# Summing four gathered corners with one tensor_reduce in place of two additions

## The reference

```python
xo = g_lt * gather(qltx, qlty) + g_rb * gather(qrbx, qrby) + g_lb * gather(qltx, qrby) + g_rt * gather(qrbx, qlty)
```

## Time and profile before

| | |
|---|---|
| times shown, us | 7589.84, 7599.73, 7600.01 |
| median, us | 7599.73 |
| span of the profiled execution, us | 7593.5 |
| busy PE / DVE / ACT / POOL, us | 5859.6 / 4572.4 / 2753.9 / 5492.1 |

### The profile page before, as it was taken

The page is one execution under the profiler, slowest core; times in us unless marked ns, Lnnn a source line. Parts: engine busy times, 40 slices in busy tenths (PEclk is TensorE's granted clock), DMA queues, the critical chain, the costliest instruction groups (busy, mean ns, idle before and its releaser), DMA issues.

```text
span 7593.5 us, 104067 instructions
## 1 busy us (share of the span) xinstructions
PE 5859.6 (77%) x33682; PEld 2811.5 (37%) x33682; DVE 4572.4 (60%) x7421; ACT 2753.9 (36%) x5357; POOL 5492.1 (72%) x5044
## 2 busy tenths in 40 slices
PE   3578787788788788888888887887888878867666
PEld 2333333334333333344334443333333433332323
DVE  3366566566666766656665666667666566755541
ACT  2333333334333343434433343333434344332322
POOL 0177777777777777777777777777777777777760
PEclk7788898899888889988888998988999888988777
DMA  2222232222322323222332223223232233312120
GB/s 88 63 71 60 57 81 72 65 82 67 84 69 70 86 68 95 64 68 76 78 81 64 83 67 84 69 68 88 65 98 64 61 82 78 81 50 66 49 65 22
DMA packets 424825, 540.78 MB, mean 71 GB/s; under 512 B 310746, under 2 KB 318974, under 8 KB 417646
## 3 DMA queue, kind: packets, MB, share of 16 engines
q0 software_dynamic: 161280, 330.62, 16.6%
q1 hardware_dynamic: 262980, 203.17, 10.4%
HBM read 404.04 MB, written 116.94 MB: 69 GB/s over the span
## 4 chain that ended last, share of the span: by engine, by line
POOL 32%; PE 31%; issue 16%; DVE 14%; ACT 5%; DMA 1%; DVEq 1%; SPq 0%; POOLq 0%; ACTq 0%
POOL gath L584 32%; PE pair L1002 10%; PE ring L940 4%; PE ring L859 3%; PE ps_def L1023 2%; ACT u L1034 2%; PE ps_acc L976 2%; DVE prod L1578 2%; DVE gath L1596 2%; ACT prod L1234 1%; DVE gath L1602 1%; PE ring L904 1%; PE ring L805 1%; PE ring L915 1%; PE ring L821 1%
## 5 line engine op out<-in xcount | busy, mean ns | idle before, releaser
L584 POOL DMA_INDIRECT gath<-table_d,idx_all x5040 | 5491.9, 1090 | 1872.7 <-issue 1871.5
L1002 PE MATMUL pair<-clamp_x,tab 128*128 128x392 f32 (+1 forms) x5760 | 2793.7, 588 | 922.7 <-DVE prod L1578 895.9
L1578 DVE SCALAR_TENSOR_TENSOR prod<-prod,pair 128x392 f32<-128x392 f32 (+1 forms) x2880 | 1629.2, 569 | 1861.0 <-PE pair L1002 1806.5
L1234 ACT ACTIVATE prod<-ps_y,y_bias 128x392 f32<-128x392 f32 (+1 forms) x2880 | 1480.9, 597 | 2250.6 <-PE ps_acc L976 2199.6
L1002 PEld LDWEIGHTS pair<-clamp_x,tab 128*128 128x128 f32 x5760 | 1044.4, 210 | 2292.1 <-DVE prod L1578 1561.1
L1596 DVE TENSOR_TENSOR gath<-gath,wgt 128x1152 f32<-128x1152 f32 x560 | 756.9, 1352 | 368.6 <-DMA gath<-table_d,idx_all 367.9
L1034 ACT ACTIVATE u<-ring 128x448 f32<-128x448 f32 (+7 forms) x1376 | 603.4, 480 | 948.5 <-PE ring L904 244.5
L976 PE MATMUL ps_acc<-prod,w_samp 128*32 128x392 f32 (+1 forms) x5760 | 649.4, 523 | 6.5 <-DVE prod L1578 6.5
L1023 PE MATMUL ps_def<-xt,w_samp 32*32 32x224 f32 x5760 | 392.8, 438 | 140.3 <-DVE xt L1611 140.3
L1554 DVE TENSOR_SCALAR clamp_x<-ps_x 128x392 f32<-128x392 f32 (+1 forms) x720 | 410.4, 570 | 103.0 <-PE ps_x L959 103.0
L940 PE MATMUL ring<-u,w 128*32 128x392 f32 x5120 | 452.7, 511 | 23.5 <-ACT u L1034 23.5
(11 more groups left out here) (155 smaller groups left out, 4109.1 us busy)
## 6 DMA issues: line engine op xcount, KB each, us to landing
gath<-table_d,idx_all POOLq DMA_INDIRECT x5040
table_d<-u SPq DMA_DIRECT2D x192, 210.0 KB
point_d<-u SPq DMA_DIRECT2D x32, 406.0 KB
u<-point_d SPq DMA_DIRECT2D x32, 406.0 KB
u<-in_x SPq DMA_DIRECT2D x8, 1568.0 KB, 7.4
x_d<-u SPq DMA_DIRECT2D x8, 1568.0 KB, 6.8
xg_d<-u SPq DMA_DIRECT2D x8, 1568.0 KB, 5.6
u<-xg_d SPq DMA_DIRECT2D x32, 392.0 KB
```

Of the source, the lines that this page charges most:

```text
L584: pool.indirect_dma_start(gath[:, k % BUFS, n * CELL:(n + 1) * CELL], None, table_d[:, :], bass.IndirectOffsetOnAxis(idx_all[:, k, n:n + 1 ...
L1002: nc.tensor.matmul(bank[:, 0:size], tab[:, b * NB + br, j * 128:(j + 1) * 128], clamp_x[:, s % 2, 0:size], start=True, stop=True)\
L1234: nc.scalar.activation(prod[:, s % 2, j, 0:size], ps_y[:, 0:size], ACT.Relu, bias=y_bias[:, j:j + 1]).then_inc(relu_ready, 1)
L1578: v.scalar_tensor_tensor(rows, rows, 1.0, bank[:, 0:size], ALU.min, ALU.mult)\
```

## The change

The two additions of a slot become one tensor_reduce over the corner axis, seen as the innermost axis of a rearranged view of the gather buffer. The sums no longer stay in the gather buffer but go to a new buffer `summed` with two halves, from which the transposition reads. A slot now has three steps on VectorE instead of four, and `weighted` counts two per slot.

```diff
+        summed = sb("summed", [128, 2, TAPS * C])
...
-                corner = gath[:, buf, :].rearrange("p (n k c) -> p n (k c)", n=TAPS, c=C)
-                low, high = corner[:, :, 0:2 * C], corner[:, :, 2 * C:]
-                dve.wait_ge(weighted, 3 * k + 1)
-                v.tensor_tensor(low, low, high, ALU.add).then_inc(weighted, 1)
+                corners = gath[:, buf, :].rearrange("p (n k c) -> p n c k", n=TAPS, c=C)
+                cell = summed[:, here % 2, :].rearrange("p (n c) -> p n c", c=C)
+                dve.wait_ge(weighted, 2 * k + 1)
+                v.tensor_reduce(cell, corners, AX.X, ALU.add).then_inc(weighted, 1)
                 yield
-                dve.wait_ge(weighted, 3 * k + 2)
-                v.tensor_tensor(high[:, :, 0:C], low[:, :, 0:C], low[:, :, C:], ALU.add).then_inc(weighted, 1)
-                yield
-                dve.wait_ge(weighted, 3 * k + 3)
+                dve.wait_ge(weighted, 2 * k + 2)
                 if here % SETS == 0:
                     wait(dve, def_full, q * (NK // SETS) + here // SETS)
                     dve.sem_inc(turn[1], 1)
-                v.transpose(xt[:, here % SETS, :].rearrange("p (n c) -> p n c", c=C), high[:, :, 0:C])\
+                v.transpose(xt[:, here % SETS, :].rearrange("p (n c) -> p n c", c=C), cell)\
                     .then_inc(xt_ready, 1)
```

## The result

The changed kernel takes **7782.7 us** (median of 4 runs, 7773.0 to 7787.4) against 7595.0 (4 runs), a ratio of 1.0239 with a 95% interval of 1.0227 to 1.0252. That is 188 us more. 7752 was forecast, with a range of 7545 to 7840 and a chance of 0.65 for slower.

A forecast was written before the change was run, and what follows sets the result against it. POOL's gather stream was taken to bound both ends, the loop of TensorE and VectorE the middle. 230 - 24.5 - 24.5 - 28.7 = +152 us on 7599.7 gave 7752 us, range 7545 to 7840.

The forecast's parts named there:

- Two paces: POOL's gather stream sets the pace in the first and last quarter, the loop of TensorE and VectorE in the middle.
- The reduce's length: On VectorE in each slot, the new reduce lasts 2.31 us, with bounds of 1.35 to 2.63.
- my low bound: For the reduce's stepped read on VectorE: 0.70 ns more for each element, giving a reduce of 2.16 us.
- POOL's relief: Gathers no longer held up by the additions: 0.35 us a slot, -24.5 us in the first and in the last quarter.
- The 28.7 us of slack: POOL gets ahead in the slower middle and uses up a buffer's free time, so the last quarter begins with -28.7 us.
- The middle: In the six middle quarters, the reduce's added time on the path costs 420 x 0.41 x 1.335 = +230 us.
- 420 x 0.41: Of the 420 slots in the middle six quarters, 41% have the reduce on the path, taken from L1602's chain share.
- The explanation of the exposed slots: In the middle, slots where TensorE waits for the third product cost 1.56 us, those with both additions on the path 1.11.
- A: Rival for the reduce: its step costs nothing, it lasts 1.35 us, the kernel takes about 7570 us; chance 0.35.
- B: Rival for the ends: POOL is held up as before, they give nothing back, about 7830 us; chance 0.06.
- C: Rival for the whole kernel: POOL's stream is the bound everywhere, 196 us come back, 7404 us; chance 0.04.

The follow-up runs named there:

- packed: The kernel before with the new buffer and both additions in one step of the weave, so three steps per slot; 7566.2 us (0.9961).
- both: The kernel before with the reduce in the first and last quarter, and two additions in one step of the weave in the middle six; 7533.8 us (0.9928).
- no_sum: The kernel before without either addition, the transposition reading corner 0 behind the weighting; 7439.1 us (0.9801).
- step4: The changed kernel with the reduce reading at a step of 4 words (16 bytes), summing other elements; 7806.3 us (one run).
- step1: The changed kernel with the reduce summing four neighbouring words in place of the four corners; 7489.5 us (ratio 0.9866 to the kernel before).
- later: The changed kernel with one empty step ahead of the reduce, putting it behind the third product and the transposition behind the fourth; 7819.7 us (1.0300).
- two_inputs_again: The changed kernel with a second weighting (two SBUF inputs) in place of the reduce, corners not summed, run again for a profile; 7823.5 us.

## Why the prediction was right

**Two paces: right for the changed kernel, and not quite for the kernel before.** The chain, VectorE's waits and the new 409.7 us of POOL's waiting in the middle say so of the changed kernel. In the kernel before, POOL is idle only for issues: its stream of gathers runs for 7027.5 us without a stop, in the middle too, at 70 x 9 x (1.101 + 0.305) = 886 us a quarter. In the runs that were profiled 336 to 343 us lie ahead of the stream and 226 to 231 behind it, so the time is the stream's. The loop of TensorE and VectorE, counted from the last transposition of one quarter to that of another, needs 889 us a quarter (5336.2 / 6): it falls 21 us behind POOL over the six, the seven buffers take that up, and in the last quarter it is made good. I took the middle's pace for the loop's alone. That doesn't matter when VectorE gets more work, but it does when it gets less: then the time falls only as far as gathers get shorter, as in packed, both and no_sum.

**The reduce's length: right in kind, 8% high.** 2.31 us from L1487's stepped write, 2.143 measured. The rate from ScalarE's copy against all 543 ns, 0.70 ns an element, my low bound, was the right one (0.69). The way in which the new read costs something was taken from writes; step4 shows that it holds.

**POOL's relief: right in kind, with one term missing.** The mean of a gather was to fall to about 1050 ns and fell to 1050. I misread in one point: the two long gathers don't end as the VectorE instruction does but 0.82 us later (2109.23 + 1.37 = 2110.60, and the weighting ends at 2109.78). The share by time that I gave comes to 0.44 us a slot and not 0.43, which changes nothing. For each end I booked 24.5 us, and the first quarter gained 11 and the last 20. The additions gave back what I had booked: counted over the trace before, the gathers that end 0.82 us behind an addition are longer than 944 ns by 21.6 us in the first quarter and by 24.6 in the last. What my sum had at nothing is the weighting. It now meets more of them at their start (63 where it was 53 in the first quarter, 58 where it was 46 in the last) and holds them up for 41.4 us in the first quarter, where it was 29.4, and for 30.5 in the last, where it was 22.7.

The 28.7 us of slack were spent in full. In the changed kernel the transposition of slot 483 ends at 6720.03, and POOL is waiting for it:

```profile
6719.55 0.48 DVE L1609 STREAM_TRANSPOSE xt<-summed 128x288 f32<-128x288 f32 x1 [0.18 <-DVE summed L1603]
...
6720.88 1.50 POOL L585 DMA_INDIRECT gath<-table_d,idx_all  x1 [1.63 <-DVE xt L1609]
```

As the window of +217.0 us runs from gather to gather, these 28 us are already in it, and it must not be held against the +230, which is a term of the loop.

**The middle: near in the sum, wrong inside.** By the last transpositions of the first and of the seventh quarter the middle grows from 5336.2 us (1201.1 to 6537.3) to 5584.1 (1197.7 to 6781.8): **+248**, where 230 was forecast. The last quarter, from there to its own last transposition, falls from 833.6 to 780.4 us, by 53.2, as much as the two terms booked for it (24.5 + 28.7). The first quarter's transposition comes only 3.4 us earlier, for 24.5. So nearly all of the 38 us by which the forecast falls short of the profiled span (+152 against +190.6) are 18 in the middle and 21 in the first quarter.

That 230 is near 248 is luck in part. With the 2.14 us that were measured my formula gives 420 x 0.41 x 1.17 = 201. The term "420 x 0.41" has the reduce on the path in 41 of 100 slots. From step1 to the changed kernel the reduce grows by 0.80 us, and the middle, from gather to gather, from 5249.2 us to 5531.9: 283 us / 420 = 0.67 us a slot, 84 of 100 (by the transpositions 290 us, 86 of 100). Against that, a reduce of 1.34 us was to cost the middle 26 to 104 us over the additions, and in step1 the middle is *shorter*, by 66 us from gather to gather (5249.2 against 5314.9) and by 43 by the transpositions. Step1's window of the middle six quarters:

```profile
1190.10:6439.30 5249.20, 4059.05 (x3781) 0.91 0.29 76
```

Two things were missing. One is that the kernel before was bound by POOL in the middle as well: there its gathers take 104 us less in step1 (4162.97 to 4059.05), and POOL waits 45 us for buffers, where it waited for none. The other is that TensorE's own work isn't constant. For the same four quarters, from the end of slot 139's transposition to that of slot 419's, in step1 and in the changed kernel:

```profile
2072.60:5602.14 3529.54, 2842.22 (x16840) 1365.20 (x16840) 2329.06 (x3425) 1376.89 (x2676) 2728.84 (x2545) 0.91 0.29 76
```

```profile
2129.12:5856.32 3727.20, 2933.22 (x16840) 1412.57 (x16840) 2560.10 (x3426) 1377.36 (x2676) 2660.60 (x2521) 0.89 0.27 71
```

The same matmuls are 91 us longer, 23 a quarter, where TensorE waits more for VectorE, and the mean granted clock is 0.89 of 2.4 GHz in place of 0.91. A quarter differs by 49 us between those two windows (198 / 4). The chain's share accounts for 0.80 x 70 x 0.48 = 27 of it (7.5% of 3668 us is 275 us, 48 of 100 slots at 2.05 us from start to start), and 23 is what TensorE's work has grown by. That the two add up so well is an argument and not a proof; no run here holds the clock still.

**The explanation of the exposed slots: not borne out.** I priced some of them at 1.56 us because the third product comes late. `later` relieves that product and is slower; as it moves the transposition too, it doesn't show what the third product alone is worth.

**The rivals.** A (the step is free) fell with the reduce's 2143 ns. Its price was wrong as well: it would have given about 7490 (step1) and not 7570, so a reduce that reads contiguously is worth far more than I gave it. B (POOL held up as before) fell with the mean of 1050 ns, C with POOL's waits in the middle. C's premise, that POOL's stream is the bound everywhere, does hold for the kernel before; what it left out is that the reduce makes the loop slower than the stream. The range of 7545 to 7840 took in A and B as well, so that the time lies in it says little; the mean of a gather, POOL's waits and the length of the reduce say more.

## What to carry to other kernels

Before several additions become one tensor_reduce over a rearranged view, look at the step of the innermost axis: 8 bytes were free here, 16 and 128 cost 60% more. One instruction in place of two can be worth more than its own time suggests, if it is of a kind that doesn't hold up the gathers that GpSimd has to issue (here tensor_reduce is, two-input additions and a tensor_scalar on SBUF aren't); and it can be worth the change only in those stretches where GpSimd sets the pace. Whether GpSimd does is best read from GpSimd itself: if it never waits for a buffer, its stream is the time, whatever the chain passes through. The share of a line on the chain of waits is what it costs now, and too low a price for work that is added to it: slots that were just off the path come onto it, and TensorE's own work grew as it waited more.

## What the runs showed of the hardware

- A gather that starts while VectorE weights or adds (two SBUF inputs) ends 0.82 us behind that instruction, and one that starts under a tensor_reduce takes 0.94 to 0.96 us (all 887 and all 901 of those that start well inside one, in the kernel before and in the changed kernel). In the mean an instruction of 1.35 us with two SBUF inputs costs the gathers 0.66 us a slot over a reduce of the same length (two_inputs_again against step1). A tensor_scalar with one SBUF input holds them up as well (12 of 12 under L1519).
- Reads in a tensor_reduce: 1341 ns at a step of 4 bytes, 1344 at 8, 2187 at 16, 2133 at 128 (medians, 1152 elements).
- The order of the same instructions among the products moves the time by 0.3 to 0.5% (packed: 25 us; later: 37 us). In the four kernels whose middle has the transposition behind the fourth product, `ps_def` takes 190 to 196 us in the four quarters shown, in the others 146 to 167. What makes it so stays open.
